# Attention with 128 small heads: outputs of two units share one bank and one turn; GpSimd does the opening's fills

## The reference, cut to what matters

```python
c_q = x @ Wq_down
c_kv = x @ Wkv_down
q_c = (c_q @ Wq_up).reshape(b, s, N_HEADS, HEAD_DIM)
q_r = (x @ Wq_rope).reshape(b, s, N_HEADS, ROPE)
k_c = (c_kv @ Wk_up).reshape(b, s, N_HEADS, HEAD_DIM)
v_c = (c_kv @ Wv_up).reshape(b, s, N_HEADS, HEAD_DIM)
k_r = x @ Wk_rope
scores = (einsum('bqhd,bkhd->bhqk', q_c, k_c) + einsum('bqhd,bkd->bhqk', q_r, k_r)) / scale
attn = softmax(scores, axis=-1)
out = einsum('bhqk,bkhd->bqhd', attn, v_c)
return out.reshape(b, s, N_HEADS * HEAD_DIM) @ Wo
```

## Time and profile before

| | us |
|---|---|
| median of 3 runs | 2463.31 (2460.43 to 2470.69) |
| the profiled execution, its time | 2466.67 |
| its span in the trace | 2464.5 |
| TensorE busy | 2415.5 (98%) |
| VectorE busy | 1573.4 (64%) |
| ScalarE busy | 1381.7 (56%) |
| GpSimd busy | 1152.5 (47%) |

### The profile page before, as it was taken

How to read it: one execution, slowest core, us unless ns; L and a number is a source line. 1 busy time by engine, 2 the same in 40 slices (tenths; PEclk the granted TensorE clock), 3 DMA queues, 4 the chain that set the end, 5 groups by cost and what they waited for, 6 DMA issues and landing times. The chain is left out here.

```text
span 2464.5 us, 39978 instructions
## 1 busy us (share of the span) xinstructions
PE 2415.5 (98%) x12184; PEld 1809.4 (73%) x12184; DVE 1573.4 (64%) x3052; ACT 1381.7 (56%) x2171; POOL 1152.5 (47%) x1153
## 2 busy tenths in 40 slices
PE   7999999999999999999999899989999999999998
PEld 4677777777777777777776588867888888888876
DVE  7666666666666666666666523277658567576577
ACT  3677777777777777777777533234325334344252
POOL 1556565656565656565655344325234343343341
PEclk9999999999999999999999999999999999999999
DMA  6222222222222222222222322120010010000100
GB/s 219 43 46 54 46 54 46 55 46 54 46 54 46 55 46 54 52 47 54 46 54 51 118 90 88 54 86 18 26 43 17 26 43 17 26 25 17 39 1 35
DMA packets 49148, 125.40 MB, mean 51 GB/s; under 512 B 6801, under 2 KB 25233, under 8 KB 42962
## 3 DMA queue, kind: packets, MB, share of 16 engines
q1 hardware_dynamic: 49106, 124.85, 19.1%
HBM read 80.27 MB, written 10.49 MB: 37 GB/s over the span
## 5 line engine op out<-in xcount | busy, mean ns | idle before, releaser
L427 DVE TENSOR_REDUCE row_max<-ps_max 128x1 f32<-128x512 f32 x1024 | 670.7, 687 | 197.7 <-PE ps_max L517 179.0
L292 POOL TENSOR_TENSOR p_parts<-probs,p_parts 128x1024 f16<-128x1024 f32 x256 | 548.0, 2150 | 370.2 <-ACT p_parts L346 370.2
L341 ACT ACTIVATE probs<-ps_score 128x1024 f32<-128x1024 f32 x512 | 523.1, 1022 | 244.9 <-PE ps_score L533 219.4
L531 PE MATMUL ps_score<-Q,K 128*128 128x512 f32 x1024 | 409.1, 400 | 4.1 <-ACT probs L341 2.1
L533 PE MATMUL ps_score<-Q,K 97*128 97x512 f32 x1024 | 406.0, 396 | 0.0
L517 PE MATMUL ps_max<-KX,Q 68*128 68x512 f32 x1024 | 378.6, 411 | 3.3 <-DVE row_max L427 3.1
L421 DVE TENSOR_TENSOR Q<-ps_x,Q 64x512 fp32r<-64x512 f32 x254 | 175.0, 689 | 222.4 <-ACT Q L336 218.7
L346 ACT ACTIVATE p_parts<-probs 128x1024 f16<-128x1024 f32 x256 | 269.5, 1053 | 4.0
L531 PEld LDWEIGHTS ps_score<-Q,K 128*128 128x128 f32 x1024 | 194.4, 190 | 69.4 <-ACT probs L341 12.1
L517 PEld LDWEIGHTS ps_max<-KX,Q 68*128 68x128 f32 x1024 | 189.0, 189 | 76.2 <-issue 28.1
L533 PEld LDWEIGHTS ps_score<-Q,K 97*128 97x128 f32 x1024 | 195.0, 190 | 38.0
(11 more groups left out here) (289 smaller groups left out, 4232.7 us busy)
## 6 DMA issues: line engine op xcount, KB each, us to landing
Q<-Q SPq DMA_DIRECT2D x64, 512.0 KB, 4.3
ffn_raw<-in_w_ffn SPq DMA_DIRECT2D x22, 768.0 KB, 4.4
w_raw<-in_w_qrope SPq DMA_DIRECT2D x32, 512.0 KB, 3.7
wq_raw<-in_wq SPq DMA_DIRECT2D x8, 1024.0 KB, 5.6
wo_raw<-in_wo SPq DMA_DIRECT2D x8, 1024.0 KB, 4.9
content_k<-probs SPq DMA_DIRECT2D x8, 512.0 KB, 6.5
Q<-content_q SPq DMA_DIRECT2D x64, 64.0 KB
K<-content_k SPq DMA_DIRECT2D x64, 64.0 KB
```

Source lines behind the costliest of these rows:

```text
L292: pool.tensor_tensor(p_lo[:, j, :, :], probs[:, j, 0:PAIRED, :], p_hi[:, j, :, :], ALU.subtract)\
L341: act.activation(probs[:, j, 2 * half:2 * half + 2, :], ps_score[half][:, :, :], ACT.Exp, scale=SCALE).then_inc(exped, 1)
L427: dve.tensor_reduce(row_max[:, j * ST + t:j * ST + t + 1], ps_max[t % 2][:, :], axis=AXX, op=ALU.max)\
L531: pe.matmul(ps_score[half][:, k, :], K1[:, b, t * P:(t + 1) * P], Q1[:, b, j, :], start=True, stop=False)
```

## The change

Two units of a group, b = 0 and b = 1, now accumulate in the same bank ps_o: the values of b = 1 stand 16 columns further right in their 32-column weights, so that its 13 used columns fall on rows of the output that b = 0 leaves zero. The bank is copied out, turned and normalised once for both, in the body of b = 0 of the next group, at the places that the lists give. In the body of b = 1 letters t and o do nothing. The normalisation's reciprocal and reduction have twice the elements, and the multiply is made twice, since the two batches go to different rows of O; o_made is counted behind the second. p0 waits for o_made in the odd units alone; in the even ones it waits for q_low. In the opening the six fills of Q2 and K2 go from VectorE's start to GpSimd, behind its set-up and ahead of L322, and GpSimd waits for them itself.

```diff
-        o_sum = buf("o_sum", [P, ST, GH, HD0])
+        o_sum = buf("o_sum", [P, ST, GH, NB, HD0])
-        recip = buf("recip", [P, ST, GH, 1])
+        recip = buf("recip", [P, ST, GH, NB, 1])
...
-                    return slot[:, b, :, :, 0:VP * HD0].rearrange(
+                    return slot[:, b, :, :, 16 * b:16 * b + VP * HD0].rearrange(
...
             pool.wait_ge(set_up, 6)
+            for b in range(NB):
+                for tile in (Q2, K2):
+                    pool.memset(tile[ROPE:P, b, :, :].bitcast(F32), 0.0).then_inc(zeros_set, 1)
+            pool.wait_ge(zeros_set, 2 * NB)
+            for b in range(NB):
+                pool.memset(K2[MROW:MROW + 1, b, :, :].bitcast(F32), 1.0).then_inc(zeros_set, 1)
+                pool.wait_ge(zeros_set, 2 * NB + b + 1)
...
-            def take_o(n):
-                act.wait_ge(pv_made, n + 1)
+            def take_o(g):
+                act.wait_ge(pv_made, 2 * g + 2)
...
-                        if kind == "t" and before:
-                            take_o(n - 1)
+                        if kind == "t" and before and b == 0:
+                            take_o(g - 1)
...
-            def normalise(g, b, n):
-                dve.wait_ge(o_turned, n + 1)
-                outs = ps_x[:, :].rearrange("p (u m) -> p u m", u=ST * GH)
+            def normalise(g):
+                dve.wait_ge(o_turned, g + 1)
+                outs = ps_x[:, :].rearrange("p (u m) -> p u m", u=ST * GH * NB)
...
-                dve.tensor_tensor(O[:, b * ST:(b + 1) * ST, bass.ds(g * GH * HD0, GH * HD0)].rearrange(
-                    "p t (h d) -> p t h d", h=GH), o_sum[:, :, :, :],
-                    recip[:, :, :, :].broadcast_to([P, ST, GH, HD0]), ALU.mult).then_inc(o_made, 1)
+                for b in range(NB):
+                    ins = dve.tensor_tensor(O[:, b * ST:(b + 1) * ST, bass.ds(g * GH * HD0, GH * HD0)].rearrange(
+                        "p t (h d) -> p t h d", h=GH), o_sum[:, :, :, b, :],
+                        recip[:, :, :, b, :].broadcast_to([P, ST, GH, HD0]), ALU.mult)
+                ins.then_inc(o_made, 1)
...
-            for b in range(NB):
-                for tile in (Q2, K2):
-                    dve.memset(tile[ROPE:P, b, :, :].bitcast(F32), 0.0).then_inc(zeros_set, 1)
-            dve.wait_ge(zeros_set, 2 * NB)
-            for b in range(NB):
-                dve.memset(K2[MROW:MROW + 1, b, :, :].bitcast(F32), 1.0).then_inc(zeros_set, 1)
...
-                        if kind == "o" and not (first and b == 0):
-                            normalise(g - 1 + b, 1 - b, n - 1)
+                        if kind == "o" and not first and b == 0:
+                            normalise(g - 1)
...
-                                  start=t == V_FIRST, stop=False)
+                                  start=t == V_FIRST and b == 0, stop=False)
...
-                                         start=False, stop=t == V_LAST and part is p_lo)
+                                         start=False, stop=t == V_LAST and part is p_lo and b == 1)
...
                             if at[0] == 0:
-                                if first:
+                                if first or b == 0:
                                     pe.wait_ge(q_low, 2 * n + 2)
                                 else:
-                                    pe.wait_ge(o_made, n - 1)
+                                    pe.wait_ge(o_made, g)
                             queries(g + b, 1 - b, 0, at[0])
...
-                        if kind == "o" and before:
-                            if more:
-                                pe.wait_ge(q_low, 2 * n + 4)
-                            else:
-                                pe.wait_ge(o_made, n - 1)
-                            turn_o(n - 1)
+                        if kind == "o" and before and b == 0:
+                            pe.wait_ge(q_low, 2 * n + 4)
+                            turn_o(g - 1)
```

More of the change, by code:

```diff
@@ L271, in part @@
                 def part(slot, k):
-                    return slot[:, b, :, :, 0:VP * HD0].rearrange("p t h (d k) -> p t h d k", k=VP)[:, :, :, :, k]
+                    return slot[:, b, :, :, 16 * b:16 * b + VP * HD0].rearrange("p t h (d k) -> p t h d k", k=VP)[:, :, :, :, k]
                 pool.tensor_copy(part(V_slot, 0), heads(PAIRED, ST - PAIRED)).then_inc(v_in, 1)
@@ L313, in _ @@
             for slot in (V_slot, V_parts):
-                pool.memset(slot[:, :, :, :, VP * HD0:VP * HD0 + 1], 1.0).then_inc(set_up, 1)
+                for b in range(NB):
+                    one = 16 * b + VP * HD0
+                    ins = pool.memset(slot[:, b, :, :, one:one + 1], 1.0)
+                ins.then_inc(set_up, 1)
             pool.memset(ident[:, :], 0.0).then_inc(set_up, 1)
@@ L413, in _ @@
             run(act, body)
-            take_o(2 * groups - 1)
+            take_o(groups - 1)
         @block.vector
@@ L428, in take_max @@
                    .then_inc(max_taken, 1)
-            def normalise(g, b, n):
-                dve.wait_ge(o_turned, n + 1)
-                outs = ps_x[:, :].rearrange("p (u m) -> p u m", u=ST * GH)
-                dve.reciprocal(recip[:, :, :, :].rearrange("p t h a -> p (t h) a"), outs[:, :, VP * HD0:VP * HD0 + 1])\
-                   .then_inc(r_made, 1)
-                dve.tensor_reduce(o_sum[:, :, :, :].rearrange("p t h d -> p (t h) d"),
+            def normalise(g):
+                dve.wait_ge(o_turned, g + 1)
+                outs = ps_x[:, :].rearrange("p (u m) -> p u m", u=ST * GH * NB)
+                dve.reciprocal(recip[:, :, :, :, :].rearrange("p t h b a -> p (t h b) a"),
+                               outs[:, :, VP * HD0:VP * HD0 + 1]).then_inc(r_made, 1)
+                dve.tensor_reduce(o_sum[:, :, :, :, :].rearrange("p t h b d -> p (t h b) d"),
                                   outs[:, :, 0:VP * HD0].rearrange("p u (d k) -> p u d k", k=VP), axis=AXX, op=ALU.add)\
                    .then_inc(r_made, 1)
-                dve.wait_ge(r_made, 2 * n + 2)
-                dve.tensor_tensor(O[:, b * ST:(b + 1) * ST, bass.ds(g * GH * HD0, GH * HD0)].rearrange(
-                    "p t (h d) -> p t h d", h=GH), o_sum[:, :, :, :],
-                    recip[:, :, :, :].broadcast_to([P, ST, GH, HD0]), ALU.mult).then_inc(o_made, 1)
+                dve.wait_ge(r_made, 2 * g + 2)
+                for b in range(NB):
+                    ins = dve.tensor_tensor(O[:, b * ST:(b + 1) * ST, bass.ds(g * GH * HD0, GH * HD0)].rearrange(
+                        "p t (h d) -> p t h d", h=GH), o_sum[:, :, :, b, :],
+                        recip[:, :, :, b, :].broadcast_to([P, ST, GH, HD0]), ALU.mult)
+                ins.then_inc(o_made, 1)
             def rope_keys(b):
@@ L486, in body @@
                             low(n + 1, 1 - b, 1)
-                        if kind == "o" and not (first and b == 0):
-                            normalise(g - 1 + b, 1 - b, n - 1)
+                        if kind == "o" and not first and b == 0:
+                            normalise(g - 1)
             run(dve, body)
-            normalise(groups - 1, 1, 2 * groups - 1)
-            dve.wait_ge(o_made, 2 * groups)
+            normalise(groups - 1)
+            dve.wait_ge(o_made, groups)
         @block.tensor
@@ L551, in outputs, with turn_o @@
                         last = pe.matmul(ps_o[32 * j:32 * (j + 1), :], V_parts[:, b, t, j, :], part[:, j, t, :],
-                                         start=False, stop=t == V_LAST and part is p_lo)
+                                         start=False, stop=t == V_LAST and part is p_lo and b == 1)
                 if t == V_LAST:
                     last.then_inc(pv_made, 1)
-            def turn_o(n):
-                pe.wait_ge(o_taken, n + 1)
+            def turn_o(g):
+                pe.wait_ge(o_taken, g + 1)
                 for t in range(ST):
@@ L669, in _ @@
                 outputs(2 * groups - 1, 1, t)
-            pe.wait_ge(o_made, 2 * groups - 1)
-            turn_o(2 * groups - 1)
+            pe.wait_ge(o_made, groups - 1)
+            turn_o(groups - 1)
 EPS = 1e-5
```

## The result

The changed kernel takes 2651.1 us, median of 4 runs (2640.6 to 2652.74), against 2461.87 for the kernel before: a ratio of 1.0752, 95% interval 1.0714 to 1.0791 (ratios here are taken over the single runs, so they are not quite the quotients of the medians). The forecast was 2465.3 with a range up to 2478. It is off by 186 us, on the side of the second rival, but ten times that rival's size.

The account below looks back on a forecast made before the run. TensorE's own sequence was taken to bound the attention stage (busy 1292.13 of 1302.40 us). Terms -5.3 + 10.2 - 3.3 + 0.4 = +2.0 us gave a median of 2465.3, range 2456 to 2478.

Parts of the forecast that it names:

- the second rival: Attention loop: the longer normalisation costs far more than 0.40 us, 0.96 per unit; +19.4 us, 2482.7; chance 0.16.
- Part 2: Even units' longer normalisation on VectorE delays the next odd unit's p0 by 0.34 us, thirty times: +10.2 us.
- E: Time added to one normalisation by longer reciprocal, longer reduction and second multiply: 0.40 us, bounds 0.27 and 0.96.
- Part 1: Odd units lose their turn (four transposes) between m22 and m23 on TensorE: 0.17 us each, 31 times, -5.3 us.
- Part 3: Opening: without fills VectorE splits x earlier, first content store at 19.4 rather than 22.68: -3.3 us.
- the rival: Opening: GpSimd's fills hold up VectorE's casts of x; +7.1 us, 2470.4, if casts wait for all fills; chance 0.08.
- Part 4: End of the attention stage: the last normalisation has no cover, so its lengthening costs +0.4 us.
- The sum: Whole kernel: -5.3 + 10.2 - 3.3 + 0.4 = +2.0 us on the profiled execution's 2466.67.

## Why the prediction was wrong

**Part 2 is the step that failed.** It said that the wait at p0 is live and that whatever lengthens the normalisation delays p0 thirty times; that held. It said that the normalisation grows by E = 0.40, of which 0.145 for a second multiply; E was 4.07 + 729.84 - 728.92 - 0.87 = 4.12. The multiply's price was taken from a row in which it starts 0.06 us ahead of GpSimd's subtraction. The 0.28 that the longer reciprocal and reduction add (729.84 - 728.92 against 0.64) carried the first multiply 0.21 us past that start, and the second then met the next subtraction. From above I had bounded E by 0.96, all three instructions doubled; no doubling covers an instruction of another engine.

For the opening I had weighed what the Trainium skill (SBUF — State Buffer, "Who interferes with whom") says of VectorE's casts, and had looked for a conflict there alone. The same section says that a VectorE instruction with two SBUF inputs contends with a GpSimd instruction that reads SBUF, and that the one issued first keeps the shared ports for its whole instruction. The runs agree for a multiply that comes second: 0.22 with one SBUF operand, 2.0 with two behind an instruction of 2.15, 1.09 behind one of half the size, 0.23 when the multiply is 0.06 us earlier. For a subtraction that comes second they show little: before, those that started just behind a multiply took 2.17 us in the median, the others 2.15.

I had also left the clock out. The wait of 3.80 us was followed by some 6 us at half clock, so that it cost 5.66 up to T. That the clock and not something else made the products slow is read from the granted clock beside them; no run kept TensorE busy through the stall, so this is not shown by an experiment.

**Part 1 held.** Without a turn, m22 to the next score takes 705.75 - 704.99 = 0.76 us (forecast 0.74, with the turn 0.91), and not the 0.48 of the slots alone. It is 0.73 to 0.76 in every such unit of the loop, and 0.90 to 0.91 before:

```profile
704.99 0.92 PE L523 MATMUL ps_max<-KX,Q 68*128 68x512 f32 x2
705.75 0.39 PE L537 MATMUL ps_score<-Q,K 128*128 128x512 f32 x1
```

**Part 3 held in its size, by another road at one place.** The first content store went at 18.82, earlier than the forecast 19.4. The fills alone gained 0.19%, 4.7 us with an interval of 0.5 to 8.9, against 3.3 forecast, and in that run's trace the first score comes at 61.8 instead of 66.3. The fills did hold the split up, as the rival had it, and it was harmless. VectorE, GpSimd and SyncE in the opening of the changed kernel:

```profile
5.57 1.25 DVE L463 CAST xh<-p_parts 128x1024 fp32r<-128x1024 f32 x1 [5.57 <-DMA p_parts<-in_xT]
6.85 1.23 DVE L465 TENSOR_TENSOR xl<-p_parts,xh 128x1024 fp32r<-128x1024 f32 x1
...
17.18 0.69 DVE L469 TENSOR_TENSOR Q<-ps_score,X 128x512 fp32r<-128x512 f32 x1 [2.23 <-ACT X L375]
...
4.47 1.80 POOL L325 MEMSET K<- 64x2048 f32 x1
6.21 2.34 POOL L325 MEMSET Q<- 64x2048 f32 x1
...
18.82 0.66 SPq L211 DMA_DIRECT2D content_q<-X  x1
```

The cast of 0.69 took 1.25 and ended 0.55 us behind the fill that ends at 6.27, as if it had stood until then; the next fill took 2.34 instead of 1.80, as if it had stood until the cast had ended. The casts met fills near their end, so a quarter lost some 0.4 us, and the first low part still waited 2.23 us for ScalarE. The subtraction at 6.85 has both operands in SBUF and runs wholly inside a fill, which only writes, and it is not stretched; before, without fills beside it, it took as long:

```profile
16.44 1.23 DVE L459 TENSOR_TENSOR xl<-p_parts,xh 128x1024 fp32r<-128x1024 f32 x1
```

So not every GpSimd instruction holds up a VectorE instruction with two SBUF operands; those that did here read SBUF.

In the profiled run of the changed kernel the first score came only 0.7 us earlier, at 65.6: TensorE's granted clock from 50 to 66.3 us was 0.50, against 0.71 before. In the run of the fills alone it was 0.69, so this isn't a property of the fills. The traces with the changed kernel's opening differ among themselves: first score at 59.1, 61.8, 62.1, 65.4 and 65.6. Why the clock differs I did not find out.

**Part 4 held.** At the stage's end, with GpSimd at rest, the normalisation takes 1552.36 + 0.36 - 1551.56 = 1.16 us; before, it took 1368.40 + 0.23 - 1367.90 = 0.73, so 0.43 more against 0.4 forecast. Its first row before:

```profile
1367.90 0.26 DVE L433 RECIPROCAL recip<-ps_x 128x16 f32<-128x16 f32 x1 [9.83 <-PE ps_x L559]
```

**The sum without the conflict** fits: the changed kernel with one operand in PSUM, where every other term is in place, took 0.18% more than the kernel before, 4.4 us with an interval of 0 to 8.9, against +2.0 forecast.

## What to carry to other kernels

Before an instruction is lengthened or moved on VectorE, lay GpSimd's timeline beside it: a VectorE instruction with two SBUF operands that stays ahead of a long GpSimd instruction reading SBUF by a few hundredths of a microsecond is priced by luck, and its own duration says nothing of what it costs a little later. Here one operand in PSUM took it out of the way, and a free stretch of a bank was enough. And where a small instruction holds a semaphore that the bounding engine waits for, the bound from above is the longest instruction that it can stand behind, once for each small instruction, and not a multiple of itself.

## What the runs showed that I had not expected

An instruction of 64 elements that normally takes 0.22 us took 2.0 to 2.17 us, with no wait shown in front of it: the time stood in its own duration, so it looks like a slow instruction and not like a stall. A delay of 0.26 us on VectorE alone made the kernel before 193 us slower. A stall of 3.80 us on TensorE was followed by 6 us at a granted clock of 0.51, which up to T cost 1.86 us more, half as much again as the stall.
